# One extra TensorE product before the first side unit of each cross-attention step

## The chip, the cores and the metric

The kernel runs on one core of a Trainium2 chip. The metric is device time in microseconds of one execution, the median of several runs. Clock figures are TensorE's granted clock as the hardware profiler records it, as a share of full speed; its two levels are 1.2 and 2.4 GHz.

## The reference

The input is a batch of 4 sequences of 512 tokens and 512 features, and a context of 4 x 1601 rows of 256 features. The first layer attends from the tokens to a projection of the context and mixes the result in with a gate. The second layer has causal self-attention (16 heads of 32), cross-attention (16 heads of 16), and two gated feed-forward experts, chosen for each token by a mask. The stage in question computes the cross-attention:

```
ci = rms_norm(hidden_states, ln_post_cross_w)
cq = heads(ci @ cq_w, NH, CHD)
ck, cv = jnp.split(encoder_outputs @ ckv_w, 2, axis=-1)      # 1601 keys
cctx = sdpa(cq, heads(ck), heads(cv), causal=False)          # softmax(cq * scale @ ck.T) @ cv
hidden_states = hidden_states + cctx @ cdense_w
```

The softmax subtracts each query's maximum score, so each score is needed twice: once for the maximum, and once, transposed, for the exponential.

## The kernel before

Seven kinds of stage follow one another on the core, with barriers between them: for each batch element memory attention, gate, norm and projections, self-attention, its dense projection, and the cross projections; then, for all four together, the cross stage (`cross_attention`) and the feed-forward.

The cross stage works through 16 groups (4 batch elements x 4 groups of 4 heads). A group has 13 steps, one for each tile of 128 keys; the last tile has 65. Step `u` is written out in TensorE's program in this order: the scores of the next step's first pair of heads (`scores(u + 1, 0)`), one side unit (`fill`), the values of the step before (`values(u - 1)`), the scores of the next step's second pair (`scores(u + 1, 1)`), and the rest of the side units that fall to this step.

- **Scores** (line 1368): two products side by side, one for each head of a pair, 49 rows (three parts of 16 and a row for the shift) by 128 keys, 512 queries wide. They go to three banks of the accumulator in turn, so they wait for the exponential two back (`s_exp`).
- **Exponentials** (line 1262): ScalarE, 128 x 512 each, four a step, from the banks of the scores into `pT_x`.
- **Values** (line 1381): four heads, each a tile of 17 columns (16 values and the sum), 128 rows, 512 wide; each stands in the trace as two records.
- **Side units.** `max`: two products side by side of 48 rows by 128 queries, 402 keys wide (line 1340), reduced by VectorE in one instruction (line 1306) over both banks. There are 32 a group, computed 12 units and one whole group ahead of the scores that need them. `turn` (line 1344): turns the maxima of a group, which then go through memory into the shift row. `dense` (lines 170 to 172, the helper `three`): six full products of 128 x 128 by 512 for the output projection, 12 of them within the steps and four at the end. Other units (`flip`, `back`, `low`) are VectorE's alone.

`cross_side_work` writes out by hand which side units fall to which step: for step `u` units are given until `ceil((u + 1) * 33 / 13)` have been. `place` numbers those that use a bank; unit `n` uses banks `2 * (n % 2)` and the next, and waits until unit `n - 2` has been read (`s_used` at least `n - 1`). VectorE takes its work in the same order (`order`). The sums of a finished group go through memory on POOL's queue (`scale_rows`) and come back to VectorE (`flip`, line 1290, a reciprocal).

`cdh`, another name for `w_hi`, holds the rounded weights of the output projection, written by ScalarE once at the start of the stage (`s_ch`). SP's queue loads keys, queries and values three groups ahead; ScalarE's and VectorE's queues issue no transfers in the stage.

Of the kernel before, what the change touches and what calls it, by code (L numbers as in the profile page):

```python
# [7 lines left out]
P = 128  # L8
# [16 lines left out]
def program(nc, t, out):  # L25
# [16 lines left out]
    with ExitStack() as keep:  # L42
# [6 lines left out]
        ps = keep.enter_context(nc.psum_tensor("ps", [P, 8, 512], f32))  # L49
# [118 lines left out]
        def three(dst, ah, al, bh, bl, start, stop, **how):  # L168

            nc.tensor.matmul(dst, ah, bh, start=start, stop=False, **how)  # L170
            nc.tensor.matmul(dst, al, bh, start=False, stop=False, **how)  # L171
            return nc.tensor.matmul(dst, ah, bl, start=False, stop=stop, **how)  # L172
# [911 lines left out]
        def cross_side_work(groups, steps, maxima, lead):  # L1084

            feed = [("max", 0, i) for i in range(maxima)] + [("turn", 0)]
            for g in range(1, groups):
                units = [("max", g, i) for i in range(maxima)]  # L1090
                feed += units[:2] + [("turn", g - 1)] * (g > 1) + units[2:]
            feed.append(("turn", groups - 1))
            first = maxima + 1 + lead
            start, feed, given, by_step = feed[:first], feed[first:], 0, []
            for u in range(groups * steps):
                g, kt = divmod(u, steps)
                now = []
                if g and kt == 4:
                    now.append(("flip", g - 1))
                if g and kt == 8:  # L1100
                    now.append(("back", g - 1))
                if g and g % 2 == 0 and kt == 11:
                    now.append(("low", g // 2 - 1))
                if g > 4 and g % 4 == 1 and kt % 3 == 0 and kt:
                    now.append(("dense", g // 4 - 1, kt // 3 - 1))
                due = -(-(u + 1) * (maxima + 1) // steps)
                while feed and given < due:
                    now.append(feed.pop(0))
                    given += 1
                by_step.append(now)  # L1110
            g = groups - 1
            by_step.append([("flip", g), ("back", g), ("low", g // 2)] + [("dense", g // 4, j) for j in range(4)])
            return start, by_step

        def cross_attention(h_all, keep_all):
# [6 lines left out]
            s = dict(zip(names.split(), sems))  # L1122
# [5 lines left out]
            start, by_step = cross_side_work(NG, KT, UNITS, 12)  # L1128
            order = start + [o for now in by_step for o in now]
            banked = [o for o in order if o[0] in ("max", "turn", "dense")]  # L1130
            place = {o: n for n, o in enumerate(banked)}
            with ctx:
# [3 lines left out]
                cd, cdh, cdl = w_raw, w_hi, w_lo  # L1136
# [10 lines left out]
                with nc.Block() as block:  # L1147
# [176 lines left out]
                    @block.tensor  # L1324
                    def _(pe):
                        def fill(o):
                            if o not in place:
                                return
                            n, g = place[o], o[1]
                            at = 2 * (n % 2)  # L1330
                            if n >= 2:
                                pe.wait_ge(s["s_used"], n - 1)
                            if o[0] == "max":
                                pair, quarter, q = o[2] % PAIRS, o[2] // PAIRS % QUARTERS, o[2] // (PAIRS * QUARTERS)
                                k0 = MAX_STARTS[quarter]
                                if o[2] == 0:
                                    pe.wait_ge(s_kq[g % RING], 16 * KQ_LOADS * (g // RING + 1))
                                for par in range(2):
                                    rows = slice(par * STEP, par * STEP + SHIFT)
                                    last = nc.tensor.matmul(ps[:, at + par, 0:MAXW], q_r[rows, g % RING, pair, q * P:(q + 1) * P],  # L1340
                                                            k_r[rows, g % RING, pair, k0:k0 + MAXW], start=True, stop=True)
                            elif o[0] == "turn":
                                pe.wait_ge(s["s_rm"], g + 1)
                                last = nc.tensor.matmul(ps[0:4 * ST, at, 0:P], row_max[:, g % 2, :], neg_ident[:, :],
                                                        start=True, stop=True)
                            else:
                                b, j = o[1], o[2]
                                cols_j = slice(j * P, (j + 1) * P)
                                pe.wait_ge(s["s_cl"], ET)
                                pe.wait_ge(s["s_low"], 2 * (b + 1))  # L1350
                                for k in range(ET):
                                    last = three(ps[:, at, :], cdh[:, k, cols_j], cdl[:, k, cols_j], ah[:, (2 * b + k) % 4, :],
                                                 al[:, (2 * b + k) % 4, :], k == 0, k == ET - 1)
                            last.then_inc(s["s_fill"], 1)

                        def scores(u, pair):

                            g, kt = divmod(u, KT)
                            k0, kn = KEY_TILES[kt]
                            if kt == 0 and pair == 0:  # L1360
                                pe.wait_ge(s["s_one"], 32)
                                pe.wait_ge(s["s_sh"], 16 * (g + 1))
                            v = 4 * u + 2 * pair
                            if v >= 2:
                                pe.wait_ge(s["s_exp"], v - 1)
                            for par in range(2):
                                rows = slice(par * STEP, par * STEP + SHIFT + 1)
                                nc.tensor.matmul(ps[0:kn, 5 + (v + par) % 3, :], k_r[rows, g % RING, pair, k0:k0 + kn],  # L1368
                                                 q_r[rows, g % RING, pair, :], start=True, stop=True).then_inc(s["s_sc"], 1)

                        def values(u):

                            g, kt = divmod(u, KT)
                            kn = KEY_TILES[kt][1]
                            pe.wait_ge(s["s_exp"], 4 * u + 4)
                            if kt == 0:
                                pe.wait_ge(s_vr[g % RING], 16 * (g // RING + 1))
                            if kt == 0 and g:
                                pe.wait_ge(s["s_ob"], g)
                            for j in range(4):  # L1380
                                last = nc.tensor.matmul(ps[j * HD:j * HD + CHD + 1, 4, :], v_r[0:kn, g % RING, kt, j, :],  # L1381
                                                        pT[0:kn, u % 3, j, :], start=kt == 0, stop=kt == KT - 1)
                            last.then_inc(s["s_pv"], 1)

                        for o in start:
                            fill(o)
                        scores(0, 0)
                        scores(0, 1)
                        for u in range(NG * KT):
                            todo = [o for o in by_step[u] if o in place]  # L1390
                            if u + 1 < NG * KT:
                                scores(u + 1, 0)
                            if todo:
                                fill(todo.pop(0))
                            if u:
                                values(u - 1)
                            if u + 1 < NG * KT:
                                scores(u + 1, 1)
                            while todo:
                                fill(todo.pop(0))  # L1400
                        values(NG * KT - 1)
                        for o in by_step[NG * KT]:
                            fill(o)
# [332 lines left out]
```

## Time and profile before

| | |
|---|---|
| three runs | 3020.84, 3036.06, 3045.57 us (median 3036.06) |
| profiled execution | 3044.3 us, its span 3041.3 us |
| mean granted TensorE clock | 0.836 |
| busy share of the span | TensorE 77%, weight loads 48%, VectorE 54%, ScalarE 31%, POOL 13% |
| TensorE products | 11966 |
| cross stage with its start | about 1738 to 2500 us |

A share is an average over stages with different limits, so it says little of one stage. Lines of the timeline give the start, the time, the engine (PE is TensorE's products, PEld its weight loads, DVE VectorE, ACT ScalarE), line, operation, result and inputs, and the number of records joined; in brackets the idle time before them and what ended it. The record of a product begins when its turn has come and ends, by a model, when the last result is out, so records overlap, and the distance from one start to the next is what the array was taken up for. Two or more tiles that work side by side in the array begin within a few ns of each other.

### The profile page before, as it was taken

The page shows a single profiled execution, that of the slowest core. Times are in us where ns is not written, and L with a number is a line of the kernel's source. Part 1 is how long each engine was busy: PE and PEld are TensorE (multiplying, and loading weights), DVE is VectorE, ACT ScalarE, POOL GpSimd, SP SyncE. Part 2 cuts the span into 40 slices and gives each one's busy share as a digit, 9 for nine tenths or more (in the row PEclk, how much of TensorE's full clock was granted, in tenths as well). Part 3 has the DMA queues.
Part 4 walks back from the last instruction along what each step waited for, and adds up shares of the span by engine and source line. Part 5 has one row for each costly group of instructions (what it writes and reads, how often), then busy time and mean ns, then how long its engine had stood idle before and what let it go on. Part 6 is the DMA issues. An engine that isn't in the chain of part 4 may idle for free. (4 is left out here: it accounts for less than half of the span.)

```text
span 3041.3 us, 32399 instructions
## 1 busy us (share of the span) xinstructions
PE 2349.0 (77%) x11966; PEld 1447.3 (48%) x11966; DVE 1633.4 (54%) x2477; ACT 944.4 (31%) x1644; POOL 381.3 (13%) x372
## 2 busy tenths in 40 slices
PE   6757858578758577775777488888888877999968
PEld 4544545354546344544544332233332315777857
DVE  3375423565442655325744377767777704766534
ACT  1211131311221212222112236756766642222101
POOL 1020002020001210020300001111111111222111
PEclk8877879787779778788868659979989958999989
DMA  2124051151161250521421724323332202333422
GB/s 82 35 84 97 15 148 51 48 131 37 64 149 35 60 122 3 121 91 35 117 65 60 129 60 93 77 39 67 65 64 48 58 10 75 91 104 104 110 76 74
DMA packets 194352, 227.67 MB, mean 75 GB/s; under 512 B 54022, under 2 KB 127626, under 8 KB 192890
## 3 DMA queue, kind: packets, MB, share of 16 engines
q1 hardware_dynamic: 187228, 217.97, 29.0%
q0 software_dynamic: 6656, 6.96, 0.9%
q8 instruction: 120, 1.97, 0.3%
q14 instruction: 60, 0.49, 0.1%
q10 hardware_dynamic: 288, 0.27, 0.0%
HBM read 163.28 MB, written 34.46 MB: 65 GB/s over the span
## 5 line engine op out<-in xcount | busy, mean ns | idle before, releaser
L1306 DVE TENSOR_REDUCE quarters<-ps 128x2 f32<-128x804 f32 x512 | 487.4, 989 | 174.8 <-PE ps L1340 173.8
L1262 ACT ACTIVATE pT_x<-ps 128x512 f32<-128x512 f32 (+1 forms) x832 | 451.2, 594 | 265.9 <-PE ps L1368 253.3
L164 DVE CAST w_hi<-w_raw 128x512 fp32r<-128x512 f32 (+2 forms) x365 | 209.1, 573 | 258.3 <-PE ps L172 147.7
L1368 PE MATMUL ps<-qx_ring,kx_ring 49*128 49x512 f32 (+1 forms) x832 | 233.7, 558 | 79.2 <-ACT pT_x L1262 78.6
L166 DVE TENSOR_TENSOR w_lo<-w_raw,w_hi 128x512 fp32r<-128x512 f32 (+2 forms) x365 | 257.7, 706 | 12.5
L1368 PEld LDWEIGHTS ps<-qx_ring,kx_ring 49*128 49x128 f32 (+1 forms) x832 | 85.6, 202 | 372.2 <-ACT pT_x L1262 319.0
L1381 PE MATMUL ps<-pT_x,vx_ring 128*17 128x512 f32 (+1 forms) x1664 | 259.9, 702 | 0.0
L1340 PE MATMUL ps<-kx_ring,qx_ring 48*128 48x402 f32 x1024 | 202.6, 428 | 55.9 <-DMA kx_ring<-cross_k_by_part 29.2
L170 PE MATMUL ps<-mi_h,w_hi 128*128 128x512 f32 (+1 forms) x440 | 175.1, 398 | 37.2 <-DVE w_lo L166 24.5
L754 ACT ACTIVATE pT_s<-ps 128x1024 f32<-128x1024 f32 (+3 forms) x128 | 88.1, 703 | 324.2 <-PE ps L840 324.1
L771 DVE TENSOR_REDUCE row_max_s<-ps 128x1 f32<-128x128 f32 (+3 forms) x256 | 123.9, 490 | 115.9 <-PE ps L810 111.8
L171 PE MATMUL ps<-mi_h,w_lo 128*128 128x512 f32 (+1 forms) x440 | 174.1, 396 | 0.0
L172 PE MATMUL ps<-mi_l,w_hi 128*128 128x512 f32 (+1 forms) x440 | 173.7, 395 | 0.0
L1340 PEld LDWEIGHTS ps<-kx_ring,qx_ring 48*128 48x128 f32 x1024 | 111.7, 215 | 119.7 <-DVE quarters L1306 82.6
L1511 POOL TENSOR_TENSOR sg<-sg,keep_all 128x512 f32<-128x512 f32 (+1 forms) x55 | 87.5, 1591 | 415.0 <-ACT sg L1492 415.0
L170 PE MATMUL ps<-xe0h,w_hi 128*128 128x512 f32 x128 | 57.0, 445 | 106.4 <-DVE w_lo L166 106.4
L810 PE MATMUL ps<-k_st,q_st 128*128 128x128 f32 (+3 forms) x256 | 126.2, 519 | 0.0
L808 PE MATMUL ps<-mask_qk,ident_b 128*128 128x128 bf16 x256 | 69.1, 270 | 64.1 <-PEq L71 47.7
L170 PEld LDWEIGHTS ps<-mi_h,w_hi 128*128 128x128 f32 (+1 forms) x440 | 82.8, 188 | 58.0 <-DVE w_lo L166 25.0
L170 PE MATMUL ps<-xh,w_hi 128*128 128x512 f32 x96 | 41.9, 436 | 78.3 <-DVE xl L272 78.3
L473 PE MATMUL ps<-sq,ones 128*128 128x512 f32 x96 | 62.2, 816 | 50.7 <-ACT sq L466 50.7
L840 PE MATMUL ps<-q_st,k_st 128*128 128x512 f32 (+3 forms) x256 | 99.3, 430 | 0.0
(263 smaller groups left out, 4409.0 us busy)
## 6 DMA issues: line engine op xcount, KB each, us to landing
kx_ring<-cross_k_by_part SPq DMA_DIRECT2D x96, 200.2 KB, 7.3
w_raw<-L_xattn_l_qkv SPq DMA_DIRECT2D x48, 256.0 KB, 2.7
w_raw<-L_xattn_v_qkv SPq DMA_DIRECT2D x48, 256.0 KB, 3.1
w_raw<-L_xattn_l_gate SPq DMA_DIRECT2D x40, 256.0 KB, 2.9
w_raw<-L_xattn_l_up SPq DMA_DIRECT2D x40, 256.0 KB, 2.9
w_raw<-L_xattn_l_down SPq DMA_DIRECT2D x40, 256.0 KB, 2.7
w_raw<-w_gate_transposed SPq DMA_DIRECT2D x32, 256.0 KB, 3.0
q_st<-rhi SPq DMA_DIRECT2D x32, 256.0 KB
```

The costliest lines, as they stand in the source:

```text
L164: nc.vector.tensor_copy(hi, raw).then_inc(s_high, 1)
L166: nc.vector.tensor_tensor(out=lo, in0=raw, in1=hi.bitcast(f32), op=ALU.subtract).then_inc(s_split, 1)
L170: nc.tensor.matmul(dst, ah, bh, start=start, stop=False, **how)
L171: nc.tensor.matmul(dst, al, bh, start=False, stop=False, **how)
L172: return nc.tensor.matmul(dst, ah, bl, start=False, stop=stop, **how)
L771: last = nc.vector.tensor_reduce(out=row_max[:, g, q, j:j + 1], in_=bank[:, 0:(q + 1) * P], axis=AX.X, op=ALU.max)
L810: last = nc.tensor.matmul(bank[:, 0:(q + 1) * P], q_st[:, hd, q * P:(q + 1) * P], k_st[:, hd, 0:(q + 1) * P], start=False, stop=True, skip ...
L1262: nc.scalar.activation(pT[0:kn, u % 3, j, :], ps[0:kn, 5 + v % 3, :], ACT.Exp, scale=SCALE)\
L1306: nc.vector.tensor_reduce(out=quarters[:, g % 2, pair, :, q, quarter], in_=ps[:, at:at + 2, 0:MAXW], axis=AX.X, op=ALU.max)\
L1340: last = nc.tensor.matmul(ps[:, at + par, 0:MAXW], q_r[rows, g % RING, pair, q * P:(q + 1) * P], k_r[rows, g % RING, pair, k0:k0 + MAXW], ...
L1368: nc.tensor.matmul(ps[0:kn, 5 + (v + par) % 3, :], k_r[rows, g % RING, pair, k0:k0 + kn], q_r[rows, g % RING, pair, :], start=True, stop=T ...
L1381: last = nc.tensor.matmul(ps[j * HD:j * HD + CHD + 1, 4, :], v_r[0:kn, g % RING, kt, j, :], pT[0:kn, u % 3, j, :], start=kt == 0, stop=kt ...
```

## The change

A helper `occupy(o)` is added to TensorE's program of the cross stage. In each step that has a banked side unit it is called between the scores of the first pair and the first of these units: it waits as the unit does for its banks, and for the first rounded weights, and multiplies 128 x 128 weights with 128 rows of 512 columns, in one pass, into the first bank of the unit that follows. That unit starts a new accumulation there. No engine reads the product, and it signals nobody. Nothing else is changed.

```diff
+                        def occupy(o):
+
+                            n = place[o]
+                            pe.wait_ge(s["s_used"], n - 1)
+                            pe.wait_ge(s["s_ch"], 1)
+                            nc.tensor.matmul(ps[:, 2 * (n % 2), :], cdh[:, 0, 0:P], cdh[:, 0, :], start=True, stop=True)
+
                         def scores(u, pair):
...
                             if u + 1 < NG * KT:
                                 scores(u + 1, 0)
                             if todo:
+                                occupy(todo[0])
                                 fill(todo.pop(0))
                             if u:
                                 values(u - 1)
```

## Rows read from the trace of the kernel before

**Rows 1.** Table by stretch: stretch, length, busy and count of each engine, clock, DMA share, GB/s.

```profile
1781.00:2428.00 647.00, 560.58 (x3314) 195.32 (x3314) 472.50 (x545) 423.53 (x784) 91.98 (x178) 0.89 0.31 60
2428.00:2496.00 68.00, 56.95 (x212) 11.82 (x212) 2.27 (x5) 37.85 (x70) 8.64 (x17) 0.50 0.03 9
```

**Rows 2.** Groups by line, 1781 to 2428: shapes, count, busy us, mean ns, idle before.

```profile
L1306 DVE TENSOR_REDUCE quarters<-ps 128x2 f32<-128x804 f32 x469 | 448.6, 990 | 145.7 <-PE ps L1340 144.7
L1262 ACT ACTIVATE pT_x<-ps 128x512 f32<-128x512 f32 (+1 forms) x764 | 414.3, 594 | 235.4 <-PE ps L1368 222.9
```

**Rows 3.** Timeline, two steps at 2.4 GHz, TensorE and its weight loads.

```profile
1936.50 0.50 PE L1368 MATMUL ps<-qx_ring,kx_ring 49*128 49x512 f32 x2 [0.49 <-ACT pT_x L1262]
1936.61 0.19 PEld L1340 LDWEIGHTS ps<-kx_ring,qx_ring 48*128 48x128 f32 x2
1936.84 0.34 PE L1340 MATMUL ps<-kx_ring,qx_ring 48*128 48x402 f32 x2
...
1937.11 1.05 PE L1381 MATMUL ps<-pT_x,vx_ring 128*17 128x512 f32 x8
...
1938.10 0.50 PE L1368 MATMUL ps<-qx_ring,kx_ring 49*128 49x512 f32 x2
...
1939.28 0.49 PE L1368 MATMUL ps<-qx_ring,kx_ring 49*128 49x512 f32 x2 [0.32 <-ACT pT_x L1262]
1939.87 0.19 PEld L1340 LDWEIGHTS ps<-kx_ring,qx_ring 48*128 48x128 f32 x2 [0.41 <-DVE quarters L1306]
1939.87 0.45 PE L1340 MATMUL ps<-kx_ring,qx_ring 48*128 48x402 f32 x2
...
1940.25 1.05 PE L1381 MATMUL ps<-pT_x,vx_ring 128*17 128x512 f32 x8
...
1942.42 0.49 PE L1368 MATMUL ps<-qx_ring,kx_ring 49*128 49x512 f32 x2 [0.50 <-ACT pT_x L1262]
```

**Rows 4.** Timeline, a dense unit at 2.4 GHz between scores and values.

```profile
2187.47 0.49 PE L1368 MATMUL ps<-qx_ring,kx_ring 49*128 49x512 f32 x2 [0.50 <-ACT pT_x L1262]
...
2187.89 0.50 PE L170 MATMUL ps<-cross_h,w_hi 128*128 128x512 f32 x1
...
2188.23 0.39 PE L171 MATMUL ps<-cross_h,w_lo 128*128 128x512 f32 x1
...
2189.16 0.40 PE L172 MATMUL ps<-cross_l,w_hi 128*128 128x512 f32 x1
...
2189.49 1.05 PE L1381 MATMUL ps<-pT_x,vx_ring 128*17 128x512 f32 x8
```

**Rows 5.** Timeline, full products of a dense unit at 1.2 GHz.

```profile
2011.98 0.63 PE L171 MATMUL ps<-cross_h,w_lo 128*128 128x512 f32 x1
...
2012.41 0.63 PE L172 MATMUL ps<-cross_l,w_hi 128*128 128x512 f32 x1
```

**Rows 6.** Timeline, two steps at 1.2 GHz: first scores and values.

```profile
1790.38 0.79 PE L1368 MATMUL ps<-qx_ring,kx_ring 49*128 49x512 f32 x2
...
1791.76 1.91 PE L1381 MATMUL ps<-pT_x,vx_ring 128*17 128x512 f32 x8
...
1795.08 0.79 PE L1368 MATMUL ps<-qx_ring,kx_ring 49*128 49x512 f32 x2 [0.35 <-ACT pT_x L1262]
...
1796.14 1.91 PE L1381 MATMUL ps<-pT_x,vx_ring 128*17 128x512 f32 x8
```

**Rows 7.** Timeline, a stalled step: VectorE's reciprocal.

```profile
1848.77 0.25 DVE L1290 RECIPROCAL rq_x<-sums_x 128x16 f32<-128x16 f32 x1 [2.84 <-DMA sums_x<-sums_by_head]
```

**Rows 8.** Table by stretch, around changes of the granted clock.

```profile
1847.00:1851.00 4.00, 1.69 (x14) 0.50 (x12) 2.23 (x4) 2.15 (x4) 0.56 (x1) 1.00 0.03 8
1916.00:1919.00 3.00, 2.50 (x22) 0.92 (x18) 2.02 (x3) 2.61 (x5) 0.00 (x0) 1.00 0.67 143
1920.00:1933.00 13.00, 12.63 (x52) 3.98 (x50) 6.83 (x9) 6.00 (x12) 0.61 (x2) 0.50 0.87 179
2258.00:2295.00 37.00, 35.19 (x140) 11.25 (x142) 19.79 (x22) 18.65 (x35) 4.00 (x8) 0.50 0.37 65
```

## The prediction

> **What bounds the kernel now.** The profiled execution took 3044.3 us: 3041.3 us of span and 3.0 us around it. The median of the three timed runs is 3036.06 us, 8.2 us less, so the sum is made on 3044.3 and 8.2 is taken off at the end. The change touches one stage only, so the first view is the table by stretch: the stage proper, in which scores, values and maxima run together, lies at 1781 to 2428 us, and behind it 68 us remain without maxima [rows 1]. In the first of them the granted clock is 0.89. The clock knows two levels, 1.2 and 2.4 GHz, so (1 - 0.89) x 2 = 22% of these 647 us, 142 us, ran at 1.2 GHz. The second view is the groups by line in the same stretch: VectorE's maxima are busy 449 us of it, ScalarE's exponentials 414 us [rows 2]. Neither fills it; TensorE is shown busy 561 us, but with modelled ends. So the order of time has to tell.
>
> The third view is two steps of the timeline at 2.4 GHz [rows 3]. TensorE goes in order: scores of the first pair, one fill, values, scores of the second pair, the remaining fills. From the second pair's scores (1938.10) to the next step's first pair (1939.28) pass 1.18 us, and TensorE idles 0.32 us of them for an exponential: this half is ScalarE's. From the first pair's scores (1936.50) to the second's (1938.10) pass 1.60 us with no idle shown in between: this half is TensorE's own, and whatever is put into it lengthens the step. The extra product is put exactly there. In the following step the fill waits for the reduction two units back (the weight load idles 0.41 us for it), and the half takes 1.95 us. Steps of the two kinds, 2.78 and 3.14 us, alternate, mean 2.96 us.
>
> **How many products.** The plan gives every step up to the 190th at least one banked unit: 483 of the 528 maxima and turns are left after the start, 33 come due every 13 steps, which uses them up in 190 or 191 steps; counted step by step it is 190. In 178 of them the first banked unit is a maximum, in 12 a dense unit. The last 18 steps have none. So 190 products of 128 x 128 by 512, once each.
>
> **What one costs at 2.4 GHz.** No product of full height stands alone between maxima in the trace, but the dense units show its pieces [rows 4]. After the scores (two tiles of 49 rows, next to each other in the array) the first product of full height begins 0.42 us later, although nothing holds it back; a maximum, of the same row tiles as the scores, begins 0.34 us later because its weights are loaded 0.11 us after the scores' start [rows 3]. Within a dense unit products follow at (2189.16 - 2188.23) / 4 = 0.23 us, but the first takes 0.34: its weights were not loaded ahead, which is 0.11 us more. Behind the last one, the values (tiles of 17 columns) begin 0.33 us after its start, 0.10 later than another full product would. I read this as: a change between row tiles, full height and column tiles makes the next weight load wait until the array has emptied. Then, from the first scores to the values:
> - step without a wait: now 1937.11 - 1936.50 = 0.61. After: 0.42 to the product, 0.11 + 0.33 to the fill, whose weights now come late too, so 0.38 to the values as in the waiting step (1940.25 - 1939.87). Sum 1.24, so +0.63 us.
> - step with the wait: now 0.97. The product waits for the same reduction as the fill did, so nothing of it hides in the wait: 0.59 + 0.44 + 0.38 = 1.41, so +0.44 us.
> Mean 0.535 us, and 178 x 0.535 = 95 us. In the 12 dense steps the following product has the same shape, so only 0.23 is added: 3 us. The lower bound for all is 0.23 us (no emptying anywhere), the upper 0.63 everywhere. I take the mean with the emptying, because the two rows next to it in kind, into and out of full height, both show it.
>
> **At 1.2 GHz.** Full products follow at 0.43 us instead of 0.23 [rows 5], and the first scores reach the values in 1.38 or 1.06 us [rows 6]. Streaming alone adds 0.20, and the scores' own streaming no longer hides behind the fill's load, so I take 0.32 us more than at 2.4 GHz, 0.85 in all. A step now takes 4.70 us there, or 0.32 less without the wait, mean 4.54; 142 / 4.54 = 31 steps, 31 x 0.32 = 10 us.
>
> **What comes back.** A few steps stall on a chain of transfers that runs in its own time: at 1847 us VectorE sits 2.84 us before a reciprocal because the sums have not landed [rows 7], and the steps at 1892, 2254 and 2373 us are of this sort; together some 7 us over their neighbours. The chain begins two or three steps earlier, and with steps 0.5 us longer it lands earlier in them: I take 4 us off. The ends of the range are 0 and 7.
>
> The work beside it costs nothing: the product reads weights made before the stage, writes a bank that is free and is overwritten by the fill behind it, and adds no semaphore signal. Its two waits are met whenever the fill's is. Behind it are queued the fill, the values and the second scores; ScalarE waits for the latter, which is the 0.535 counted. VectorE gets 0.5 us more per step and was no bound. DMA keeps the engines 0.31 busy in the stage, and SP, POOL and ACT issue what they did.
>
> **The clock.** A step at 1.2 GHz costs 4.54 instead of 2.96 us, so the 142 us hold 31 x 1.58 = 49 us that a steady 2.4 GHz would return. The granted clock fell after a stall in which TensorE was busy 1.69 of 4 us, but also after a stretch in which it was busy 2.50 of 3, at the end of a group where the key tile has 65 rows; one stay at 1.2 GHz lasted 37 us [rows 8]. The product adds 0.23 us of streaming but lengthens the step by 0.53, so the busy share of a step hardly moves: I expect about the same share at the lower level, less what the vanished stalls would have set off, 5 us.
>
> The Trainium skill's page "TensorE: Matmul & The Clock Gate" (Why this matters for your kernels) advises keeping TensorE busy and avoiding idle gaps because these return it to the lower clock. The fall behind the busy 2.50 of 3 us shows that here the absence of a gap did not suffice.
>
> **Sum:** 95 + 3 + 10 - 4 - 5 = 99 us; 3044.3 + 99 = 3143, less 8.2: 3135 us. I say 3132.
>
> **Rivals.**
> 1. The product is cheap: weights are loaded ahead whatever the shapes, and it costs its streaming, 0.23 us, 0.43 at 1.2 GHz. 190 x 0.23 + 31 x 0.20 = 50 us, so 3086. For it: the loads inside a dense unit and of the first fill are ahead [rows 3, 4]. Against: the 0.42 and 0.33 at both ends of the dense unit. Chance 0.12. The Trainium skill (same page, Back-to-back issue gap) gives the distance of 512 columns as N/2.4 + 2.5 ns, 216 ns; by it the 190 products would cost 41 us at the higher clock. The rows' 0.23 agrees inside a run of equal shapes.
> 2. The product costs what I say, but a full-height product each step holds the clock up, or brings it back sooner: 99 + 5 - 49 - 10 = +45 us, 3081. For it: the falls at the 65-row tiles look marginal, and the stretch without maxima stayed at 1.2 GHz for its whole 68 us [rows 1], so the added maxima do matter. Against: the longer step. Chance 0.18.
> 3. Not slower. One mechanism, the clock between 1781 and 2496 us: if it stays at 2.4 GHz in the main part (49 us back) and also behind it, where 17 steps of about 4 us could run near two ScalarE halves of 1.18 us each (17 x 1.68 = 28 us), 77 us come back. It decides from the point at which a product costs less than 77 / 190 = 0.41 us; at 0.23 the sum is 44 - 77 = -33 us, 3003, and without the part behind, -5 - 4 = -9, 3027. Both the clock and the cheap product are needed for a clear gain. Chance 0.08.
> 4. More falls: every step has more changes of shape with empty array, so the clock is lost more often. If the share at 1.2 GHz doubles, some 40 steps go from 3.50 to about 5.39 us: +76, 3210. Chance 0.12.
> That the product would not run at all, or alongside the scores, I leave within rival 1: it has the full height and width of the array and its own issue.
> The forecast has 0.50.
>
> **Range and chances.** 3075 to 3195 us: the lower end takes in rivals 1 and 2, the upper my case with 0.63 everywhere (178 x 0.095 = 17 more) and part of rival 4. About 0.17 lies outside. A measurement tells about 1%, 30 us, from no change. Slower by over 1% are the forecast, rivals 1, 2 and 4, less their tails: 0.90. Within 1%: 0.07, half of rival 3 and those tails. Faster: 0.03.
>
> **What would show it.** TensorE has 12156 products; a new group of 190. In steps at 2.4 GHz, first scores to product 0.42 or 0.59, product to fill 0.44, fill to values 0.38 in both kinds of step; steps of 3.41 and 3.58 us. If product to fill shows 0.23, rival 1 holds. The granted clock over the stage near 0.89, the stage about 100 us longer; near 1.00 is rival 2 or 3, below 0.8 rival 4. VectorE's idle time before the maxima grows by about what the stage grows. The other stages keep their lengths. The prediction is wrong if the half from the second to the first scores changes from 1.18 us, or if maxima wait less for VectorE because the product filled their wait.

## The result and the profile after

The changed kernel took 3125.55 us in the median against 3032.4 us before; the ratio is 1.026 (95% interval 1.0173 to 1.0348), some 79 us. Run again unaltered it took 3091.25 us in the median, ratio 1.0151 (1.0107 to 1.0195), some 46 us. The two intervals just overlap; the change makes the kernel slower by 1.5 to 2.6%, and the forecast was 3132 us in a range of 3075 to 3195. The ratios leave out slow executions: in the first result that of 3465.02 us, which is also the profiled one, and in the second those of 3119.06 and 3130.54 us. So the profile shown is of the second time, 3092.55 us with a span of 3090.7 us; the plain medians of that time lie 61 us apart.

The table by stretch, for the part with products and the part behind it (stretch, length, busy and count of TensorE, its weight loads, VectorE, ScalarE and POOL, granted clock, DMA share, GB/s), answers to [rows 1]:

```profile
1778.00:2492.00 714.00, 628.64 (x3502) 229.73 (x3502) 482.26 (x542) 423.00 (x782) 92.00 (x178) 0.94 0.28 54
2492.00:2538.00 46.00, 34.88 (x194) 8.58 (x194) 2.52 (x5) 35.40 (x66) 8.63 (x17) 0.87 0.05 13
```

Counted from the same step (it begins at 1783 us before, 1779 after), the part with products grew from 645 to 713 us, by 68. Its granted clock rose from 0.89 to 0.94: the time at 1.2 GHz fell from 144 to 88 us. The part behind it took 42 us up to the start of its last step where it had taken 60, because in this execution the clock stayed at 2.4 GHz for 34 of its 46 us. Before the stage (1778 against 1783 us) and behind it (552 against 549) little moved. Groups of the part with products, answering to [rows 2], and the new one:

```profile
L1306 DVE TENSOR_REDUCE quarters<-ps 128x2 f32<-128x804 f32 x468 | 456.5, 994 | 207.4 <-PE ps L1340 202.3
L1262 ACT ACTIVATE pT_x<-ps 128x512 f32<-128x512 f32 (+1 forms) x762 | 413.5, 594 | 278.3 <-PE ps L1375 264.6
...
L1361 PE MATMUL ps<-w_hi 128*128 128x512 f32 x190 | 99.3, 523 | 8.5 <-DVE quarters L1306 1.9
```

190 products; VectorE's idle time before the maxima grew from 146 to 207 us, as the step waits for TensorE. Two steps of the timeline, answering to [rows 3]:

```profile
1928.85 0.50 PE L1375 MATMUL ps<-qx_ring,kx_ring 49*128 49x512 f32 x2 [0.50 <-ACT pT_x L1262]
1929.28 0.19 PEld L1361 LDWEIGHTS ps<-w_hi 128*128 128x128 f32 x1 [0.24 <-issue]
1929.28 0.50 PE L1361 MATMUL ps<-w_hi 128*128 128x512 f32 x1
1929.71 0.18 PEld L1340 LDWEIGHTS ps<-kx_ring,qx_ring 48*128 48x128 f32 x2 [0.25 <-issue]
1929.71 0.45 PE L1340 MATMUL ps<-kx_ring,qx_ring 48*128 48x402 f32 x2
...
1930.09 1.05 PE L1388 MATMUL ps<-pT_x,vx_ring 128*17 128x512 f32 x8
...
1931.07 0.50 PE L1375 MATMUL ps<-qx_ring,kx_ring 49*128 49x512 f32 x2
...
1932.25 0.50 PE L1375 MATMUL ps<-qx_ring,kx_ring 49*128 49x512 f32 x2 [0.32 <-ACT pT_x L1262]
1932.84 0.19 PEld L1361 LDWEIGHTS ps<-w_hi 128*128 128x128 f32 x1 [0.41 <-DVE quarters L1306]
1932.85 0.49 PE L1361 MATMUL ps<-w_hi 128*128 128x512 f32 x1
...
1933.27 0.45 PE L1340 MATMUL ps<-kx_ring,qx_ring 48*128 48x402 f32 x2
...
1933.65 1.05 PE L1388 MATMUL ps<-pT_x,vx_ring 128*17 128x512 f32 x8
...
1935.82 0.50 PE L1375 MATMUL ps<-qx_ring,kx_ring 49*128 49x512 f32 x2 [0.50 <-ACT pT_x L1262]
```

In the first step the product begins 0.43 us after the scores, the fill 0.43 after it, the values 0.38 later: 1.24 us where it had been 0.61. In the second, 0.60, 0.42 and 0.38: 1.40 where it had been 0.97. The steps take 3.40 and 3.57 us. The weights of the product, and of the fill behind it, are loaded only when their turn has come (1929.28 and 1929.71), where before the fill's were loaded 0.11 us after the scores' start, while these streamed [rows 3]. The half from the second scores to the first is still 1.18 us. At 1.2 GHz (starts of scores, product, fill, values of one step):

```profile
1967.16 0.79 PE L1375 MATMUL ps<-qx_ring,kx_ring 49*128 49x512 f32 x2
...
1967.90 0.79 PE L1361 MATMUL ps<-w_hi 128*128 128x512 f32 x1
...
1968.63 0.70 PE L1340 MATMUL ps<-kx_ring,qx_ring 48*128 48x402 f32 x2
...
1969.26 1.91 PE L1388 MATMUL ps<-pT_x,vx_ring 128*17 128x512 f32 x8
```

### The profile page after: what moved, and what is told of

Same layout as the page of the kernel before. It is cut to its first block and busy times, and to the rows that moved or that the text cites. A ratio compares the mean times of both kernels' runs of the same rounds, so it can differ in the third digit from the quotient of the medians.

```text
span 3463.2 us, 32969 instructions
## 1 busy us (share of the span) xinstructions
PE 2824.5 (82%) x12156; PEld 1576.9 (46%) x12156; DVE 1639.9 (47%) x2477; ACT 946.1 (27%) x1644; POOL 381.4 (11%) x372
## 5 line engine op out<-in xcount | busy, mean ns | idle before, releaser
L164 DVE CAST w_hi<-w_raw 128x512 fp32r<-128x512 f32 (+2 forms) x365 | 198.5, 544 | 371.2 <-PE ps L172 265.0
L1388 PE MATMUL ps<-pT_x,vx_ring 128*17 128x512 f32 (+1 forms) x1664 | 292.6, 793 | 0.0
L1340 PE MATMUL ps<-kx_ring,qx_ring 48*128 48x402 f32 x1024 | 220.5, 464 | 42.6 <-DMA kx_ring<-cross_k_by_part 27.3
L170 PE MATMUL ps<-mi_h,w_hi 128*128 128x512 f32 (+1 forms) x440 | 202.1, 459 | 37.2 <-issue 27.5
L171 PE MATMUL ps<-mi_h,w_lo 128*128 128x512 f32 (+1 forms) x440 | 201.5, 458 | 0.0
L172 PE MATMUL ps<-mi_l,w_hi 128*128 128x512 f32 (+1 forms) x440 | 201.2, 457 | 0.0
L170 PE MATMUL ps<-xe0h,w_hi 128*128 128x512 f32 x128 | 67.5, 528 | 106.3 <-DVE w_lo L166 106.3
L362 PE MATMUL ps<-pT,cs 128*128 128x512 f32 (+1 forms) x208 | 130.4, 769 | 0.0
L1361 PE MATMUL ps<-w_hi 128*128 128x512 f32 x190 | 105.0, 553 | 9.9 <-DVE quarters L1306 2.3
L473 PE MATMUL ps<-sq,ones 128*128 128x512 f32 x96 | 71.7, 923 | 50.6 <-ACT sq L466 50.6
```

Source lines behind the costliest of these rows:

```text
L164: nc.vector.tensor_copy(hi, raw).then_inc(s_high, 1)
L362: last = nc.tensor.matmul(ps[:, e, :], cs[0:kn, kt, e * P:(e + 1) * P], pT[0:kn, kt % 3, :], start=kt == 0, stop=kt == KT - 1)
```

## Experiments

Times are set against the kernel before, run on the same chip in the same rounds.

**The same kernel again**, for the profile and a better figure of the whole.

> The changed kernel again, unaltered, to have more times and a profile. My theory: a product between row tiles and the fill costs 0.63 us in a step without a wait and 0.44 in one with it, because the array empties before and after each change of shape: first scores to product 0.42 or 0.59, product to fill 0.44, fill to values 0.38; about 95 us over 190 products, total 70 to 110 us over before. Rival A (only the streaming counts): product to fill 0.23 us, total about 50 us. Rival B (the product holds the clock at 2.4 GHz): the mean granted clock from the first to the last product is above 0.95 and the total about 45 us over before.

Measured: +46 us (ratio 1.0151, 1.0107 to 1.0195), where 70 to 110 was expected. Every distance in a step is as expected, 0.43 or 0.60, 0.43, 0.38. The total is not: it lies at rival B's figure, though the clock, 0.94, stays under the 0.95 that rival B asked for. So the price of a product is settled, and the clock gave part of it back.

**Row tiles in place of full height.** No change of shape is left around the product.

```diff
-                            nc.tensor.matmul(ps[:, 2 * (n % 2), :], cdh[:, 0, 0:P], cdh[:, 0, :], start=True, stop=True)
+                            for par in range(2):
+                                r = slice(par * STEP, par * STEP + SHIFT)
+                                nc.tensor.matmul(ps[:, 2 * (n % 2) + par, :], cdh[r, 0, 0:P], cdh[r, 0, :], start=True, stop=True)
```

> The full-height product is replaced by two side by side of 48 rows by 128 columns, 512 wide, of the same shape as the scores and the fill around it (into the two banks of the fill). My theory: no change of shape is left, so each step pays 0.23 us of streaming: first scores to product 0.34, product to fill 0.23, 45 to 55 us over before. Rival A (streaming is all that ever counted, or an issue cost): as slow as the changed kernel itself. If the clock needs the full height to be held up, the clock of the stage is lower here than in the changed kernel; if it needs only busy time, the same.

Measured: ratio 0.9989 (0.9956 to 1.0022), 3 us under before, where 45 to 55 over was expected. One step of its timeline, and the table for the part with products:

```profile
1911.81 0.50 PE L1377 MATMUL ps<-qx_ring,kx_ring 49*128 49x512 f32 x2 [0.50 <-ACT pT_x L1262]
1911.91 0.19 PEld L1363 LDWEIGHTS ps<-w_hi 48*128 48x128 f32 x2
1912.15 0.39 PE L1363 MATMUL ps<-w_hi 48*128 48x512 f32 x2
...
1912.38 0.34 PE L1340 MATMUL ps<-kx_ring,qx_ring 48*128 48x402 f32 x2
...
1912.65 1.05 PE L1390 MATMUL ps<-pT_x,vx_ring 128*17 128x512 f32 x8
...
1913.63 0.50 PE L1377 MATMUL ps<-qx_ring,kx_ring 49*128 49x512 f32 x2
```

```profile
1764.00:2420.00 656.00, 565.61 (x3688) 212.24 (x3688) 472.91 (x542) 422.56 (x782) 92.01 (x178) 0.96 0.31 59
```

The price is the expected one: 0.34 to the product, 0.23 to the fill, 0.27 to the values, so 0.84 us, 0.23 more than before, and the product's weights are loaded ahead (1911.91). What was not expected is that the clock pays for it: 0.96, 51 us at 1.2 GHz in place of 144, and the part takes 656 us, 11 more than before. That is not the luck of one profile: the mean clock of all ten executions is 0.857 to 0.866, that of the 17 before on this chip 0.827 to 0.851.

**A narrow product.** Full height, 64 columns instead of 512: the emptying stays, the streaming goes.

```diff
-                            nc.tensor.matmul(ps[:, 2 * (n % 2), :], cdh[:, 0, 0:P], cdh[:, 0, :], start=True, stop=True)
+                            nc.tensor.matmul(ps[:, 2 * (n % 2), 0:64], cdh[:, 0, 0:P], cdh[:, 0, 0:64], start=True, stop=True)
```

> The product keeps its full height but streams 64 columns instead of 512, 0.03 us instead of 0.21. My theory: the two changes of shape stay, so a step still pays about 0.44 us without a wait and 0.25 with it, 55 to 70 us over before. Rival A (streaming is the cost): under 10 us over before.

Measured: ratio 1.0513 (1.0449 to 1.0578), +155 us, where 55 to 70 was expected: the smallest product makes the slowest kernel.

```profile
1969.25 0.51 PE L1375 MATMUL ps<-qx_ring,kx_ring 49*128 49x512 f32 x2 [0.35 <-ACT pT_x L1262]
...
1969.68 0.30 PE L1361 MATMUL ps<-w_hi 128*128 128x64 f32 x1
...
1969.91 0.45 PE L1340 MATMUL ps<-kx_ring,qx_ring 48*128 48x402 f32 x2
...
1970.29 1.05 PE L1388 MATMUL ps<-pT_x,vx_ring 128*17 128x512 f32 x8
...
1971.28 0.50 PE L1375 MATMUL ps<-qx_ring,kx_ring 49*128 49x512 f32 x2
```

```profile
1774.00:2572.00 798.00, 732.26 (x3502) 271.09 (x3502) 477.76 (x543) 422.01 (x781) 92.01 (x178) 0.73 0.25 49
```

At 2.4 GHz it is as expected: 1.04 us to the values, 0.43 over before, steps of 3.20 and 3.37 us. But the granted clock is 0.73: 437 of 798 us run at 1.2 GHz, three times as long as before, and the mean clock of all four executions is 0.787 to 0.808. The product adds 0.43 or 0.23 us to a step and only 64 columns of streaming, and the clock goes down. Rival A falls with the distances. The number of products is the same as in the changed kernel, so it does not set the clock; what differs is how much streaming each adds for the time that it adds.

**Two products.** The second follows in the same shape.

```diff
                             nc.tensor.matmul(ps[:, 2 * (n % 2), :], cdh[:, 0, 0:P], cdh[:, 0, :], start=True, stop=True)
+                            nc.tensor.matmul(ps[:, 2 * (n % 2), :], cdh[:, 0, 0:P], cdh[:, 0, :], start=True, stop=True)
```

> The full product twice in a row. My theory: the second has the shape of the first and follows at 0.23 us, so 44 us more than the changed kernel plus 6 for the steps at 1.2 GHz, 130 to 155 us over before. If each product paid its own emptying, it would be 190 us over before. If more activity holds the clock up, the stage's granted clock is higher than in the changed kernel and it is under 120.

Measured: ratio 1.0294 (1.0236 to 1.0351), +89 us, 43 more than the single product on the same chip, near the 50 expected for the second; the whole misses its 130 to 155 because the first product does, and lies under the 120 named for a clock that is held up.

```profile
1931.60 0.50 PE L1376 MATMUL ps<-qx_ring,kx_ring 49*128 49x512 f32 x2 [0.32 <-ACT pT_x L1262]
...
1932.19 0.50 PE L1361 MATMUL ps<-w_hi 128*128 128x512 f32 x1
...
1932.53 0.40 PE L1362 MATMUL ps<-w_hi 128*128 128x512 f32 x1
...
1932.85 0.45 PE L1340 MATMUL ps<-kx_ring,qx_ring 48*128 48x402 f32 x2
...
1933.23 1.05 PE L1389 MATMUL ps<-pT_x,vx_ring 128*17 128x512 f32 x8
```

```profile
1768.00:2508.00 740.00, 651.91 (x3690) 244.06 (x3688) 483.45 (x542) 421.90 (x780) 92.03 (x178) 0.97 0.27 52
```

From the first product to the second pass 0.34 us, to the fill 0.32, in all 1.63 us from the scores to the values against 1.40: 0.23 for the second, as expected. The clock is 0.97, 38 us at 1.2 GHz against 88 with one product, so part of that comes back as well.

**The full product where TensorE idles**, in ScalarE's half, before the first scores, into the bank that these use next. The edit, against the kernel before:

```diff
+                        def occupy(u):
+                            v = 4 * u
+                            pe.wait_ge(s["s_exp"], v - 2)
+                            pe.wait_ge(s["s_ch"], 1)
+                            nc.tensor.matmul(ps[:, 5 + v % 3, :], cdh[:, 0, 0:P], cdh[:, 0, :], start=True, stop=True)
...
                             if u + 1 < NG * KT:
+                                if todo:
+                                    occupy(u + 1)
                                 scores(u + 1, 0)
                             if todo:
                                 fill(todo.pop(0))
```

> The same full product, 190 times, but in ScalarE's half of the step: after the last fill and before the first scores, into the bank that these scores use next, once its old content has been read. Theory: the price depends on the place. TensorE idles 0.32 or 0.50 us there at 2.4 GHz, and emptying, product and emptying take about 0.5, so a step grows by 0.0 to 0.1 us and not by 0.53; the step keeps its length with more streaming in it, so the time at 1.2 GHz between the first and last product falls below the 144 us of before, and the total lies 35 to 5 us under before. Rival (the product costs 0.5 us wherever it stands): 45 us or more over before, as the changed kernel.

Measured: ratio 0.9923 (0.9884 to 0.9962), 23 us under before.

```profile
1929.59 0.50 PE L1375 MATMUL ps<-qx_ring,kx_ring 49*128 49x512 f32 x2
...
1929.92 0.35 PE L1340 MATMUL ps<-kx_ring,qx_ring 48*128 48x402 f32 x2
...
1930.20 1.05 PE L1388 MATMUL ps<-pT_x,vx_ring 128*17 128x512 f32 x8
...
1931.18 0.50 PE L1375 MATMUL ps<-qx_ring,kx_ring 49*128 49x512 f32 x2
...
1931.52 0.53 PE L1340 MATMUL ps<-kx_ring,qx_ring 48*128 48x402 f32 x4
...
1931.98 0.50 PE L1361 MATMUL ps<-w_hi 128*128 128x512 f32 x1
...
1932.41 0.50 PE L1375 MATMUL ps<-qx_ring,kx_ring 49*128 49x512 f32 x2
```

```profile
1779.00:2392.00 613.00, 590.71 (x3497) 217.63 (x3497) 471.85 (x542) 422.00 (x781) 92.00 (x178) 0.97 0.33 63
```

The same 190 products, and a step takes 2.82 us (1929.59 to 1932.41) in place of 2.78, its neighbour 3.09 in place of 3.14. The clock is 0.97, 41 us at 1.2 GHz, and the part takes 613 us in place of 645. VectorE still waited for the sums in this stretch, 9 times and 13.1 us in all, so the clock does not need these stalls to go. The product goes from -23 to +46 us or more by its place alone.

**One row tile there.** As before, with 48 rows.

```diff
-                            nc.tensor.matmul(ps[:, 5 + v % 3, :], cdh[:, 0, 0:P], cdh[:, 0, :], start=True, stop=True)
+                            nc.tensor.matmul(ps[:, 5 + v % 3, :], cdh[0:SHIFT, 0, 0:P], cdh[0:SHIFT, 0, :], start=True, stop=True)
```

> As the run before, but the product has 48 rows, one row tile of the shape of the fill. Theory: no change of shape and all of it in idle time: a step at 2.4 GHz keeps its 2.78 or 3.14 us. If busy time alone holds the clock, the time at 1.2 GHz falls as with the full product, total 35 to 10 us under before. If the number of busy rows matters, it falls less or not at all, total within 10 us of before.

Measured: ratio 0.989 (0.9847 to 0.9933), 33 us under before.

```profile
1763.00:2375.00 612.00, 563.11 (x3501) 216.92 (x3501) 471.87 (x543) 422.16 (x781) 92.02 (x178) 0.97 0.33 63
```

The steps keep their 2.78 and 3.14 us, and the clock is as high as with the full product, 42 us at 1.2 GHz in this execution.

**Only behind the maxima.** No product in the 190 steps, but one in each of the last 18, between scores and values; once full, once as two row tiles.

```diff
+                            if not todo:
+                                occupy(("dense", NG // 4 - 1, 0))
                             if todo:
                                 fill(todo.pop(0))
```

> No product in the 190 steps; instead the full product in each of the last 18 steps, those without maxima, between first scores and values. Before, these ran at 1.2 GHz at 4.04 us each. Theory (busier steps keep the clock): they run at 2.4 GHz at about 3.0 us, 15 us under before for the whole. Rival (emptying dilutes it): the clock still falls and they take about 4.9 us, 15 us over before.

> As the run before, with two row tiles side by side of 48 rows in place of the full product, no change of shape. Theory: 2.4 GHz and about 2.65 us a step, 20 to 25 us under before. Rival (not enough activity): 1.2 GHz and about 4.5 us, 7 us over before.

Measured: ratio 0.9963 (0.9929 to 0.9997), 11 us under before, with the full product, and 0.9992 (0.9951 to 1.0032), 2 us under, with row tiles. The tables for the last part, full product first:

```profile
2416.00:2489.00 73.00, 62.51 (x210) 15.51 (x208) 2.52 (x5) 34.52 (x64) 8.64 (x17) 0.53 0.03 8
```

```profile
2421.00:2474.00 53.00, 41.92 (x237) 11.54 (x236) 2.51 (x5) 36.24 (x68) 8.64 (x17) 0.84 0.05 11
```

With the full product the clock stayed at 1.2 GHz for all but two short stretches, and a step took 4.77 us in place of 4.04: in this execution it went as the rival says. But it was the second longest of ten (3045.70 us, clock 0.840), and the whole, faster by 1 to 22 us, speaks against the rival's 15 us over before and for the theory's 15 under; what the other nine did in the last steps is not seen. With row tiles the clock came up to 2.4 GHz after 10 us for three steps, fell, and was back for the last eight, at 2.83 us a step; the part took 12 us less than before in this execution, and the whole does not reach the 20 to 25 expected. So neither pair of theory and rival is decided. In both kernels the part with maxima is that of the kernel before, and it gives two more figures for it: 641 and 645 us, 130 and 138 of them at 1.2 GHz.

**All steps, in the idle half**, first the row tile, then the full product; the condition `if todo` is left out.

```diff
-                                if todo:
-                                    occupy(u + 1)
+                                occupy(u + 1)
```

> The row tile of 48 rows in ScalarE's half, now in all steps, the 17 without maxima too, where TensorE has more idle time. Theory (free where TensorE idles, and busy time holds the clock): the main part as with the row tile before, about 612 us; behind it, if one row tile a step is enough, 2.4 GHz and about 2.4 us a step instead of 4.04, 25 us more gained, 60 to 40 us under before in all. Rival (too little activity without maxima, since half the rows are idle): the last steps stay at 1.2 GHz and the total is that of the row tile in 190 steps, 40 to 20 us under before.

> The full product in ScalarE's half in all steps. In the last 17 steps the idle time of a half at 2.4 GHz is about 0.8 us, more than emptying, product and emptying take, so a step keeps about 2.4 us. Theory: 2.4 GHz held for some or all of them, 50 to 35 us under before. Rival: they fall to 1.2 GHz as with the full product in TensorE's half and the total is that of the full product in 190 steps, 35 to 20 under before.

Measured: the row tile 0.9908 (0.9878 to 0.9938), 28 us under before and no gain over the 190 steps alone; the full product 0.9852 (0.9805 to 0.9898), 45 us under before, the fastest kernel of this study. The two parts of the row tile, the last part of the full product and one step there:

```profile
1781.00:2405.00 624.00, 578.97 (x3503) 222.34 (x3502) 472.02 (x544) 422.43 (x782) 92.01 (x178) 0.93 0.32 62
2405.00:2469.00 64.00, 59.87 (x209) 14.54 (x206) 2.24 (x5) 35.14 (x66) 8.63 (x17) 0.50 0.04 9
```

```profile
2379.00:2422.00 43.00, 38.84 (x224) 11.23 (x226) 1.85 (x4) 36.62 (x68) 8.64 (x17) 1.00 0.06 14
```

```profile
2381.19 0.50 PE L1375 MATMUL ps<-qx_ring,kx_ring 49*128 49x512 f32 x2 [0.25 <-ACT pT_x L1262]
...
2381.62 1.05 PE L1388 MATMUL ps<-pT_x,vx_ring 128*17 128x512 f32 x8
...
2382.60 0.50 PE L1375 MATMUL ps<-qx_ring,kx_ring 49*128 49x512 f32 x2
...
2383.03 0.50 PE L1361 MATMUL ps<-w_hi 128*128 128x512 f32 x1
...
2383.79 0.50 PE L1375 MATMUL ps<-qx_ring,kx_ring 49*128 49x512 f32 x2 [0.26 <-ACT pT_x L1262]
```

One row tile leaves the last steps at 1.2 GHz. The full product holds 2.4 GHz through all of them, at 2.60 us a step, where the same product in TensorE's half (3.11 us in the one step mostly at that level) lost it in its profiled execution. The part with maxima takes 608 us with the full product. With the row tile it takes 624 us, 81 of them at 1.2 GHz, where the same 190 steps with the same product took 612 and 42 in the run above; this execution was the longest of its ten. So one profile can be some 40 us at 1.2 GHz off another of the same work.

In one table, parts as profiled once each:

| kernel | steps at 2.4 GHz, us | at 1.2 GHz in the part with maxima, us | this part, us | whole, against before |
|---|---|---|---|---|
| before | 2.78 / 3.14 | 144 | 645 | |
| only behind, full / row tiles | 2.78 / 3.14 | 130 / 138 | 641 / 645 | 0.996 / 0.999 |
| changed | 3.40 / 3.57 | 88 | 713 | 1.026, again 1.015 |
| row tiles | 3.01 / 3.37 | 51 | 656 | 0.999 |
| narrow | 3.20 / 3.37 | 437 | 798 | 1.051 |
| double | 3.64 / 3.80 | 38 | 741 | 1.029 |
| full, idle half | 2.83 / 3.09 | 41 | 613 | 0.992 |
| row tile, idle half | 2.78 / 3.14 | 42 | 612 | 0.989 |
| row tile, idle half, all steps | 2.78 / 3.14 | 81 | 624 | 0.991 |
| full, idle half, all steps | 2.83 / 3.09 | 28 | 608 | 0.985 |

## Why the prediction was right, and where it was not

**Which half the product falls into.** Right, and it decides the sign. From second to first scores still 1.18 us, all of the price between first and second; the same product in the other half costs nothing and gains.

**The price of one.** Right to 0.02 us in each step shown. Expected from the first scores to the values 1.24 and 1.41, measured 1.24 and 1.40; steps of 3.41 and 3.58 expected, 3.40 and 3.57 measured. The mean of the steps of common length at 2.4 GHz rose from 2.99 (140 of them) to 3.49 us (155), by 0.50 where the sum had 0.535, since more than half of the steps are of the kind that waits. The split is shown from both sides: without the changes of shape a product costs 0.23 us in either step, with hardly any streaming 0.43 and 0.23. Two changes are 1.24 - 0.84 = 0.40 us where nothing is waited for, 0.20 each: 0.43 - 0.34 and the 0.11 of the late weights before the product, 0.43 - 0.23 behind it. That the array empties in this time is a reading; what the rows show is that the next weights are not loaded ahead across a change of shape. Rival 1 fell. By the distance of 216 ns that the Trainium skill gives ("TensorE: Matmul & The Clock Gate", Back-to-back issue gap) the estimate for 190 products is 41 us. The trace agrees with it inside one shape, as the row tiles show with 0.23 us, and not across a change, where the same 512 columns take 0.43.

**At 1.2 GHz.** The step of 0.74, 0.73 and 0.63 us to the values, 2.10 in all, is 0.72 over the 1.38 of before [rows 6]. All steps wholly at this level take 5.39 us in the mean (ten of them) where they took 4.56 (21), 0.83 more; the sum had 0.85.

**Stalls.** Right in kind: VectorE's waits for the sums in this part were 9.2 us over 6 times before and are gone, and the steps that had stalled at 1848 [rows 7], 1892 and 2373 us run at the common length. The step at 2254 us was read wrongly. Its stall is not the sums but ScalarE, which waits 2.33 us for `att_pairs` to land before it rounds the context (line 1249); that wait is still there after the change, 1.32 us, and the step takes 4.10 us. By the steps' lengths some 5 us went, near the 4 of the sum.

**The clock.** This is the term that was mis-sized, and its sign is wrong. The sum had 10 us for the dearer steps at 1.2 GHz less 5 for vanished falls, so the clock to stay about where it was. In the profile the time at 1.2 GHz fell from 144 to 88 us. What it cost before is 144 x (1 - 2.99 / 4.56) = 50 us over a steady 2.4 GHz; after, 88 x (1 - 3.49 / 5.39) = 31 us. So the clock gave some 19 us back instead of taking 5 (some 14 if one starts from the 130 us of the kernel with products only behind the maxima). With 178 x 0.50 + 12 x 0.23 = 92 for the products, 92 - 19 - 5 = 68, which is what the part grew by. The forecast's argument was that a longer step with a little more streaming has the same busy share. The experiments show that small differences there moved this stage's clock a long way in either direction: the narrow product (less streaming for the time it adds) tripled the time at 1.2 GHz, the row tiles and the double product (more) took away two thirds of it and more. For the single product a second cause is not set apart: the two falls that followed a stall before, at 1851 us for 10 us and at 2257 for 38, have no counterpart after, while falls behind the tiles of 65 rows remain (at 1966 us TensorE had been busy 2.50 of 3 us, as in [rows 8]). The forecast gave these vanished falls 5 us.

**Luck in the two totals.** The median of 3125.55 us lies close to the forecast of 3132 in part by luck: the four values behind it include the one of 3465.02 us, and the ratio says +79 us where the sum had 99. Rival 2 (45 us) had the direction of the clock, and its total is that of the repeat, but for another reason: it let all of the 144 us come back, where 56 did, and the execution profiled gained 18 us behind the maxima that are in no term of it.

**Why the two results differ.** Both kernels are the same, and what lies between them is time at 1.2 GHz. From the mean clock and the span of each execution, (1 - clock) x 2 x span, the four that count in the first result (3087 to 3130 us) had 864 to 1007 us at that level, 939 in the mean, and the four of the second (3073 to 3092 us) 835 to 878, 856 in the mean. A microsecond at 1.2 GHz costs 1 - 3.49 / 5.39 = 0.35 us in this stage, so 83 us more are an estimate of 29 us, and the means of the times lie 29 us apart. The kernel before had 894 to 1004 us, 958 in the mean, on the chip of the second result. So in the first result the clock seems to have given little back, and the +79 us lie nearer the bare price, 92 less 5. Where in the kernel those executions lost the clock is not known, since none of them was profiled, nor why it differs between the two.

**What varies.** The part behind the maxima was at 2.4 GHz for 34 us in the profile of the changed kernel, for some 9 in that with row tiles and for 1 in that with two products; it is worth 18 us, and no product stands in it. Whether the products before it had a share in that is not shown. It makes most of the difference between a part that grew by 68 us and a span that grew by 49. How often it happens was not measured.

**Not slower** (rival 3) was wrong for this place. With the product in the idle half its mechanism is what the profile shows: with all steps, the part with maxima is 37 us shorter and the part behind it 21, and the steps at 2.4 GHz pay nothing in the mean (2.83 and 3.09 us in place of 2.78 and 3.14).

## What to carry to other kernels

Work that is read by nobody can pay for itself through TensorE's clock. Here it gained only in time in which TensorE waits for another engine; find that time by the step's halves and not by the busy share. Before adding a product between others, look at their tile shapes: a change between row tiles, full height and column tiles kept the next weights from being loaded ahead and cost 0.20 us each here, with weights of 128 columns. In a stage whose clock already goes up and down, cost a change once with the clock falling and once with it rising: kernels that differ by one small product a step had between 28 and 437 us at 1.2 GHz here. And take more than one profile before a difference of some 40 us at that level is put down to an edit.

## What the hardware showed that was not expected

- The least work cost the most: 64 columns instead of 512 made the kernel 155 us slower than before instead of 46, because the granted clock of the part fell from 0.89 to 0.73.
- One row tile of 48 rows in idle time cut the time at 1.2 GHz beside the maxima (to 42 and 81 us in two executions, from 130 to 144), as 128 rows did (to 41 and 28). Without the maxima the row tile did not, and only the full product in the shorter step was at 2.4 GHz for the whole length, in one execution.
